# Where VectorE turns blocks of adj, and when norm and x rows are handled, in a four-layer graph network

## The chip, the cores and the metric

One core of a Trainium2 chip runs the whole program. The metric is the device time of one execution in microseconds (us); the number given is the median of several runs.

## The reference

Inputs are x (4096 x 256) and a sparse matrix adj (4096 x 4096), all float32. Four layers each compute x = layernorm(x + layer(x, adj)):

- Layer 0 is attention with 4 heads of 64 columns. `scores = q k^T / 8 + graph_bias * adj`, set to -1e9 where adj is 0, softmax over the row, times v, then an output projection.
- Layer 1 is graph attention with leaky ReLU and a softmax over the edges.
- Layers 2 and 3 multiply by adj scaled by its row sums on both sides, and by a weight matrix.

Layers 2 and 3 need adj transposed, as operand of TensorE. The kernel makes that copy, adjT, in HBM while layer 0 runs.

## The kernel before, in words

The change touches layer 0 (`layer0_attention`, L149 to L974) alone. The rows of the output are cut into 16 chunks of 256 rows (`CT` = 2 tiles of 128). A chunk has 4 heads; a head has 8 beats (`BEATS`), one for each piece of 128 rows by 1024 columns of scores. Four beats are a side (`SIDE`), so a chunk has 8 sides of 4 beats, 32 beats. A pair (side, r) names a beat: side 0 to 7, r 0 to 3. The order of all engines is written out by hand in terms of these pairs, and each engine has its own program:

- **TensorE** (`tensor_program`, L640): in a side it makes the scores of four pieces, 12 beats ahead of their use (L579), turns four pieces of finished probabilities by a multiplication with the identity (L592), and at the end of the side multiplies the turned pieces by the values (`aggregate`, L605, 32 matmuls). In sides with half = 0 it projects the output of the head before (L614). In side 3 it turns the x rows of the next chunk (`turn_x`, L550) and sides 1, 3, 5 and 7 include, for every second head, the making of q (L559). Scores and turned pieces share three PSUM places of two banks in turn; the scores of step r = 0 have to be read before the second turned piece of the side can be written, those of r = 1 before the third scores.
- **VectorE** (`vector_program`, L931): at each beat it reads one piece of scores (`read_scores`, L865: scale, add bias, row maximum, written to SBUF). After it, by (side, r), come the other jobs: at r = 1 the sum of a finished head is inverted, at r = 3 the projected rows are added to `acc` (`add_step`, L903), in sides 4 to 6 the bias of the next chunk is made (`MAKE_BIAS`, L816 and L827/L829), and blocks of adj are turned (`turn_block`, L885).
- **ScalarE** takes the exponential (L716), copies turned pieces out of PSUM (L725) and issues the loads of the values, two of 256 KB a side (L766).
- **GpSimd** (POOL) makes the masks for the bias of the next chunk (L502), takes the power in the layer norm (L129) and stores the finished rows x1 (L494).
- **SyncE** (SP) issues, in the order of its program, the loads of blocks (L393), four stores for each turned block (L403), the loads of x rows (L470, L473) and, at beats 12 to 19 of a chunk, the eight loads of the next chunk's bias of 512 KB each (L382).

**Blocks.** adj is cut into 256 blocks of 128 rows by 512 columns (256 KB). A block is loaded to one of four places (`squares`), turned in place by VectorE in squares of 32 x 32, and written to adjT by four DMAs of 64 KB in pieces of 128 bytes. `BLOCKS_AT` says how many blocks are turned after the read of the beat (side, r); its counts sum to 17 a chunk, so chunk 15 has one block left. SP handles a block one beat behind VectorE (`store_turned`): it waits until block b is turned, issues the four stores, waits until the stores of block b-1 have landed and issues the load of block b+3:

```
for b in blocks_in(c, side, r):
    store_block(b)
    if b + 3 < BLOCKS:
        wait(sync, block_stored[(b + 3) % BLOCK_PLACES], ...)
        load_block(b + 3)
```

**Norm and acc.** When the last head of chunk c-1 has been added at (0, 3) of chunk c, VectorE takes the statistics of `acc` (`ln.statistics`), POOL the power, VectorE normalises in place (`ln.normalise`), and POOL stores the rows. Then `start_acc(c)` (L887) waits for that store and for the x rows of chunk c, and sets acc to x + bo. Behind it SP loads the x rows of chunk c+1 into the same tile `xs`; TensorE turns them in side 3. After that `xs` serves as mask of two wide pieces of bias and is loaded once more in side 7.

Of the kernel before, what the change touches and what calls it, by code (L numbers as in the profile page):

```python
# [39 lines left out]
def wait(eng, sem, value):  # L40

    if isinstance(value, int) and value <= 0:
        return
    eng.wait_ge(sem, value)
# [104 lines left out]
def layer0_attention(nc, shared, x, adj, Wqkv, bqkv, Wout, bout, graph_bias, v_heads, value_stored, x1, x1_stored, adjT):  # L149
# [48 lines left out]
    SCORE_STEP = (0, 2, 5, 7)  # L198
    TURN_STEP = (1, 3, 4, 6)
    SIDE_STEPS = 2 * SIDE  # L200
    BLOCKS_AT = {(0, 1): 1, (0, 3): 2, (1, 3): 3, (2, 1): 1, (2, 3): 2, (3, 1): 1, (3, 3): 1, (6, 3): 2, (7, 1): 1, (7, 3): 3}
    CHUNK_BLOCKS = sum(BLOCKS_AT.values())
    WIDE = (3, 6)
    NARROW = tuple(i for i in range(BEATS) if i not in WIDE)
    x_tiles, adj_tiles, x1_tiles, w_rows = tiles_of(x), tiles_of(adj), tiles_of(x1), tiles_of(Wqkv)
    with ExitStack() as ctx:
# [13 lines left out]
        acc = sp.sb("acc", [P, CT, D])  # L220
# [10 lines left out]
        ln = LayerNorm(sp, CT)  # L231
# [59 lines left out]
        acc_ready = sp.sem("acc_ready")  # L291
# [28 lines left out]
        def x_loads(c, first):  # L320

            return 16 * (2 * c + 1) if c == 0 or not first else 16 * 2 * c

        def is_first(c, h):
            return isinstance(c, int) and c == 0 and h == 0
# [5 lines left out]
        def blocks_in(c, side, r):  # L331

            before = sum(n for slot, n in BLOCKS_AT.items() if slot < (side, r))
            first = CHUNK_BLOCKS * c + before
            return [b for b in range(first, first + BLOCKS_AT.get((side, r), 0)) if b < BLOCKS]

        pool_of_places = (turn_bank[1], turn_bank[0], score_bank)

        def score_place(side, r):

            return pool_of_places[(SIDE_STEPS * side + SCORE_STEP[r]) % 3]
# [5 lines left out]
        def sides():  # L347

            return ((h, half, 2 * h + half, SIDE * half) for h in range(H) for half in range(2))
# [17 lines left out]
        def unit_after(c, h, ahead):  # L367

            return c + (h + ahead) // H, (h + ahead) % H
# [5 lines left out]
        def sync_program(sync, early):  # L375
# [4 lines left out]
            def load_bias(c, i):  # L380
                t, pp = piece_at(i)
                sync.dma_start(bias[:, t:t + 1, pp * PIECE:(pp + 1) * PIECE],  # L382
                               adj_tiles[:, bass.ds(c * CT + t, 1), pp * PIECE:(pp + 1) * PIECE])\
                    .then_inc(adj_loaded[i], 16)
# [62 lines left out]
            def store_turned(c, side, r):  # L447
# [4 lines that stand above are left out]
                        wait(sync, block_stored[(b + 3) % BLOCK_PLACES], 16 * SQUARES * ((b + 3) // BLOCK_PLACES))  # L452
                        load_block(b + 3)

            def body(c, last):
                for h, half, side, j0 in sides():
                    for r in range(SIDE):
                        at = BEATS * h + j0 + r
                        if r:
                            store_turned(c, side, r - 1)  # L460
                        elif side:
                            store_turned(c, side - 1, SIDE - 1)
                        elif c:
                            store_turned(c - 1, SIDES - 1, SIDE - 1)
                        if last:
                            early(sync, at)
                            continue
                        if h == 1 and half == 0 and r == 2:
                            sync.wait_ge(acc_start, CT * (c + 1))
                            sync.dma_start(xs[:], x_tiles[:, bass.ds((c + 1) * CT, CT), :]).then_inc(x_loaded, 16)  # L470
                        if h == H - 1 and half == 1 and r == 1:
                            wait(sync, wide_used, len(WIDE) * (c + 1))
                            sync.dma_start(xs[:], x_tiles[:, bass.ds((c + 1) * CT, CT), :]).then_inc(x_loaded, 16)  # L473
                        if BIAS_LOAD <= at < BIAS_LOAD + BEATS:
                            i = at - BIAS_LOAD
                            sync.wait_ge(score_read, CHUNK_BEATS * c + (H - 1) * BEATS + i + 1)
                            load_bias(c + 1, i)
            chunks(sync, body)

        def gpsimd_program(pool):  # L480
# [301 lines left out]
        def vector_program(dve, early):  # L782
# [104 lines left out]
            def start_acc(c):  # L887

                wait(dve, x1_stored, 16 * c)
                dve.wait_ge(x_loaded, x_loads(c, False))  # L890
                for t in range(CT):
                    dve.tensor_tensor(acc[:, t, :], xs[:, t, :], bo[:], ALU.add).then_inc(acc_start, 1)
# [38 lines left out]
            def body(c, last):  # L931
                for h, half, side, j0 in sides():
                    s = H * c + h
                    before = unit_after(c, h, -1)
                    has_before = not is_first(c, h)
                    G = SIDES * c + side
                    for r in range(SIDE):
                        j = j0 + r + AHEAD
                        if not (last and h + j // BEATS >= H):
                            read_scores(*unit_after(c, h, j // BEATS), j % BEATS, score_place(G, r))  # L940
                        if r == 1:
                            if half == 1:
                                invert_sums(s, h % 2)
                            if side == 1 and has_before and c:
                                dve.wait_ge(acc_ready, s)
                                ln.statistics(dve, acc, c - 1)
                            if side == 2:
                                start_acc(c)
                        if r == 3:
                            if half == 0 and has_before:  # L950
                                add_step(s - 1, before[1], before[1] % 2, before[0])
                            if side == 1 and c:
                                ln.normalise(dve, acc, c - 1)
                            if half == 1 and h % 2 and not (last and h + 3 >= H):
                                for e in range(2):
                                    finish_q(*unit_after(c, h, 3), e)
                        if (side, r) in MAKE_BIAS and not last:
                            i = MAKE_BIAS[side, r]
                            if i in WIDE:
                                make_wide_bias(c + 1, i)  # L960
                            else:
                                make_bias(c + 1, i)
                        for b in blocks_in(c, side, r):
                            turn_block(b)
                        if last:
                            early(dve, SIDE * side + r)
            chunks(dve, body)
            final = UNITS - 1
            add_step(final, H - 1, (H - 1) % 2, CHUNKS - 1)
# [1054 lines left out]
```

## Time and profile before

| | us |
|---|---|
| median of 3 runs | 3180.06 (3180.02 to 3185.33) |
| the profiled execution | 3181.8 |
| its span | 3180.1 |
| TensorE matmul busy | 2997.9 (94%) |
| TensorE weight loads busy | 2212.2 (70%) |
| VectorE busy | 2115.4 (67%) |
| ScalarE busy | 1893.3 (60%) |
| GpSimd busy | 764.6 (24%) |

The profile records one execution. A busy time counts instructions at work; matmuls are pipelined, so a busy TensorE need not be at its peak. Idle time in front of an instruction is put down to what released it. The granted clock is the share of TensorE's full clock that the chip gave. DMA share is the mean busy share of the 16 DMA engines. Layer 0 takes about the first 1760 us of the span, the other layers the rest.

### The profile page before, as it was taken

How to read it: one execution, taken by the hardware profiler on the slowest of the kernel's cores; microseconds unless marked ns; L12 is line 12 of the kernel's file. 1: busy time of each engine (PE TensorE's matmuls, PEld its weight loads, DVE VectorE, ACT ScalarE, POOL GpSimd, SP SyncE). 2: the span in 40 equal slices, each digit the busy share in tenths (PEclk: the TensorE clock that was granted, in tenths of full speed). 3: DMA queues.
4: the chain of work that ended last, by engine and by line, in shares of the span. 5: the costliest groups of instructions: out<-in, count | busy, mean ns of one | idle time of the engine just before them, and what ended most of it. 6: DMA issues, size and time to landing. Idle time of an engine off the chain costs nothing.

```text
span 3180.1 us, 45294 instructions
## 1 busy us (share of the span) xinstructions
PE 2997.9 (94%) x16612; PEld 2212.2 (70%) x16612; DVE 2115.4 (67%) x3607; ACT 1893.3 (60%) x2705; POOL 764.6 (24%) x454
## 2 busy tenths in 40 slices
PE   8898999999999999998999899999999999999998
PEld 6676777776777677776777555555547888788887
DVE  6677767776777677766775797777734554664554
ACT  3666667666666667666767477777754333443332
POOL 2123312331133113321330145555530110000000
PEclk9999999999999999999999999999999999999999
DMA  6788797789787978797775533334248999899882
GB/s 185 145 159 173 174 178 163 173 176 186 157 178 175 189 161 175 168 204 146 170 167 128 206 144 120 146 119 146 84 106 194 217 201 204 212 214 215 204 197 65
DMA packets 725868, 534.42 MB, mean 168 GB/s; under 512 B 565776, under 2 KB 605968, under 8 KB 709264
## 3 DMA queue, kind: packets, MB, share of 16 engines
q1 hardware_dynamic: 682464, 445.00, 61.3%
q10 hardware_dynamic: 36288, 66.08, 8.6%
q0 software_dynamic: 6896, 20.45, 2.2%
q8 instruction: 133, 2.18, 0.3%
q14 instruction: 87, 0.71, 0.1%
HBM read 443.29 MB, written 88.08 MB: 167 GB/s over the span
## 4 chain that ended last, share of the span: by engine, by line
PE 60%; DMA 13%; DVE 12%; SPq 7%; issue 5%; ACT 2%; POOL 1%; DVEq 0%; POOLq 0%; ACTq 0%
PE gl_four L1474 11%; PE gl_quad L1527 7%; PE gl_quad L1528 7%; PE gl_quad L1529 7%; PE at_o L605 5%; DMA adjT<-at_probs 5%; PE at_turn L579 5%; SPq L403 5%; PE at_turn L592 5%; DVE at_probs L865 4%; DMA at_probs<-in_adj 4%; PE gl_quad L1457 3%; PE at_score L579 3%; DVE at_bias L816 2%; PE at_score L592 2%
## 5 line engine op out<-in xcount | busy, mean ns | idle before, releaser
L716 ACT ACTIVATE at_probs<-at_probs,at_minus_max 128x1024 f32<-128x1024 f32 x512 | 581.7, 1139 | 10.7 <-DVE at_minus_max L870 9.8
L725 ACT ACTIVATE at_pT<-at_turn 128x1024 f32<-128x1024 f32 x342 | 346.1, 1024 | 308.8 <-PE at_turn L592 308.6
L865 DVE CUSTOM_DVE_ANT_0 at_probs<-at_turn,at_bias 128x1024 f32<-128x1024 f32 x336 | 409.0, 1220 | 164.2 <-PE at_turn L579 158.3
L502 POOL TENSOR_SCALAR at_masked<-at_bias 128x512 bf16<-128x512 f32 x180 | 374.2, 2093 | 582.2 <-DMA at_bias<-in_adj 535.1
L605 PE MATMUL at_o<-at_pT,at_values 128*64 128x256 f32 x4096 | 470.3, 382 | 0.0
L1474 PE MATMUL gl_four<-gl_early,gl_first_wh 128*128 128x512 f32 x1024 | 462.5, 595 | 6.4 <-ACT gl_early L1595 6.4
L1620 ACT ACTIVATE gl_split<-gl_units 128x1024 fp32r<-128x1024 f32 x256 | 263.8, 1055 | 278.6 <-PE gl_quad L1529 278.6
L592 PE MATMUL at_turn<-all_ident,at_probs 128*128 128x128 f32 x2736 | 366.8, 281 | 56.0 <-DVE at_maxima L865 53.6
L579 PE MATMUL at_turn<-at_kT,at_q 128*128 128x512 f32 x1344 | 403.8, 423 | 10.0 <-DVE at_maxima L865 10.0
L1527 PE MATMUL gl_quad<-gl_split,gl_rows_hi 128*128 128x512 f32 x1024 | 402.4, 393 | 4.7 <-DVE gl_split L1808 4.6
L605 PEld LDWEIGHTS at_o<-at_pT,at_values 128*64 128x64 f32 x4096 | 282.5, 137 | 172.8 <-issue 43.2
L1528 PE MATMUL gl_quad<-gl_split,gl_rows_hi 128*128 128x512 f32 x1024 | 398.5, 389 | 0.0
L1529 PE MATMUL gl_quad<-gl_split,gl_rows_lo 128*128 128x512 f32 x1024 | 398.5, 389 | 0.0
L592 PEld LDWEIGHTS at_turn<-all_ident,at_probs 128*128 128x128 f32 x2736 | 327.0, 145 | 101.9 <-DVE at_maxima L865 68.5
L1808 DVE TENSOR_TENSOR gl_split<-gl_units,gl_split 128x1024 fp32r<-128x1024 f32 x256 | 306.3, 1222 | 116.4 <-ACT gl_split L1620 116.0
L1474 PEld LDWEIGHTS gl_four<-gl_early,gl_first_wh 128*128 128x128 f32 x1024 | 185.2, 191 | 192.4 <-issue 185.2
L885 DVE STREAM_TRANSPOSE at_probs<-at_probs 128x512 f32<-128x512 f32 x256 | 175.5, 700 | 207.7 <-DMA at_probs<-in_adj 206.6
L1170 POOL TENSOR_SCALAR gl_first_weights<-gl_first_weights 128x1024 f32<-128x1024 f32 x57 | 237.2, 4162 | 267.6 <-ACT gl_first_weights L1577 267.6
L579 PEld LDWEIGHTS at_turn<-at_kT,at_q 128*128 128x128 f32 x1344 | 233.0, 193 | 74.7 <-issue 30.7
L865 DVE CUSTOM_DVE_ANT_0 at_probs<-at_score,at_bias 128x1024 f32<-128x1024 f32 x176 | 214.7, 1220 | 90.1 <-PE at_score L579 87.0
L725 ACT ACTIVATE at_pT<-at_score 128x1024 f32<-128x1024 f32 x170 | 174.0, 1024 | 154.9 <-PE at_score L592 154.9
L1527 PEld LDWEIGHTS gl_quad<-gl_split,gl_rows_hi 128*128 128x128 f32 x1024 | 192.3, 188 | 46.6 <-DVE gl_split L1808 6.8
(135 smaller groups left out, 3838.0 us busy)
## 6 DMA issues: line engine op xcount, KB each, us to landing
gl_units<-adjT SPq DMA_DIRECT2D x512, 256.0 KB, 7.8
at_bias<-in_adj SPq DMA_DIRECT2D x128, 512.0 KB, 7.1
at_probs<-in_adj SPq DMA_DIRECT2D x256, 256.0 KB, 4.9
adjT<-at_probs SPq DMA_DIRECT2D x1024, 64.0 KB, 4.4
gl_first_weights<-in_adj SPq DMA_DIRECT2D x32, 2048.0 KB, 8.2
at_values<-v_heads ACTq DMA_DIRECT2D x252, 256.0 KB, 5.1
gl_early<-x SPq DMA_DIRECT2D x160, 128.0 KB, 2.6
x<-gl_early POOLq DMA_DIRECT2D x64, 128.0 KB, 2.7
```

The lines of the kernel that those rows point to most:

```text
L502: pool.tensor_scalar(masked[:, g % MASKS, :], part, 0.0, MASKED / SCALE, ALU.is_equal, ALU.mult)\
L579: last = pe.matmul(place[:, at], q[:, q_place(h), part, t * P:(t + 1) * P], kT[:, h, col:col + BANK], start=part == 0, stop=part == 1)
L592: last = pe.transpose(place[:, a * CN + t * P:a * CN + (t + 1) * P], ring[:, place_in_ring(s, m // BEATS), t, m % BEATS * P:(m % BEATS + 1 ...
L605: last = pe.matmul(o_bank[side * HD:(side + 1) * HD, 0:CN], values[:, q, a, :], pT[:, slot, a % GROUP * CN:(a % GROUP + 1) * CN], start=q ...
L716: act.activation(part, part, ACT.Exp, bias=minus_max[:, k, t:t + 1], scale=1.0, accum_out=sums[:, k, t, pp:pp + 1]).then_inc(prob_ready, 1)
L725: act.activation(pT[:, j % PT_SLOTS, :], place[:], ACT.Copy).then_inc(pT_ready, 1)
L865: dve.tensor_tensor_reduce(out=ring[:, place_in_ring(u, pp), t, :], in0=place[:], in1=bias[:, t, at], scale=SCALE, scalar=LOWEST, op0=ALU. ...
L1474: last = pe.matmul(out_bank1[c % 2][half], wh[:, m * D + half * P:m * D + (half + 1) * P], pT[:, g % PT_RING, part * CN:(part + 1) * CN], ...
L1527: pe.matmul(out_bank3[r % 2][half], rows_hi[:, at], block_hi, start=first, stop=False)
L1528: pe.matmul(out_bank3[r % 2][half], rows_hi[:, at], block_lo, start=False, stop=False)
L1529: last = pe.matmul(out_bank3[r % 2][half], rows_lo[:, at], block_hi, start=False, stop=final)
L1808: dve.tensor_tensor(split3[:, slot, 1, :], tiles[:, n, part:part + 2 * CN], split3[:, slot, 0, :].bitcast(F32), ALU.subtract).then_inc(lo3 ...
```

## The change

It gives `BLOCKS_AT` one block a beat on 17 beats, where it had one to three blocks on ten; the sum stays 17. VectorE's statistics of the finished chunk go from (1, 1) to (0, 3), the normalising from (1, 3) to (1, 1), the start of acc from (2, 1) to (2, 0). SP's load of the next chunk's x rows goes from (2, 2) to (2, 1). The condition `has_before and c` becomes `c`, which is the same for the chunks in question. The loads of the values are as they were, two of 256 KB a side.

```diff
-    BLOCKS_AT = {(0, 1): 1, (0, 3): 2, (1, 3): 3, (2, 1): 1, (2, 3): 2, (3, 1): 1, (3, 3): 1, (6, 3): 2, (7, 1): 1, (7, 3): 3}
+    BLOCKS_AT = {(0, 0): 1, (0, 2): 1, (1, 0): 1, (1, 2): 1, (2, 1): 1, (2, 2): 1, (2, 3): 1, (3, 0): 1, (3, 1): 1, (3, 2): 1, (4, 0): 1, (4, 2): 1, (5, 0): 1, (6, 3): 1, (7, 0): 1, (7, 1): 1, (7, 2): 1}
...
-                        if h == 1 and half == 0 and r == 2:
+                        if h == 1 and half == 0 and r == 1:
                             sync.wait_ge(acc_start, CT * (c + 1))
                             sync.dma_start(xs[:], x_tiles[:, bass.ds((c + 1) * CT, CT), :]).then_inc(x_loaded, 16)
...
                         if r == 1:
                             if half == 1:
                                 invert_sums(s, h % 2)
-                            if side == 1 and has_before and c:
-                                dve.wait_ge(acc_ready, s)
-                                ln.statistics(dve, acc, c - 1)
-                            if side == 2:
-                                start_acc(c)
+                            if side == 1 and c:
+                                ln.normalise(dve, acc, c - 1)
+                        if r == 0 and side == 2:
+                            start_acc(c)
                         if r == 3:
                             if half == 0 and has_before:
                                 add_step(s - 1, before[1], before[1] % 2, before[0])
-                            if side == 1 and c:
-                                ln.normalise(dve, acc, c - 1)
+                            if side == 0 and c:
+                                dve.wait_ge(acc_ready, s)
+                                ln.statistics(dve, acc, c - 1)
```

## Rows read from the trace of the kernel before

**Rows 1.** By stretch: start:end, length; busy PE, PEld, DVE, ACT, POOL; clock; DMA share; GB/s.
```profile
201.80:1678.50 1476.70, 1362.08 (x9352) 1048.39 (x9352) 1041.35 (x1932) 1006.21 (x1472) 370.92 (x196) 0.97 0.83 173
730.90:835.20 104.30, 94.71 (x668) 72.58 (x668) 74.59 (x138) 71.74 (x105) 24.78 (x14) 1.00 0.86 176
```
**Rows 2.** Waits from 100 to 1690 us: us in total, times, longest us.
```profile
PE at_turn L592 <- DVE at_maxima L865: 53.6, 24, 4.6
PE at_mixed L550 <- DMA at_xs<-in_x: 28.6, 14, 4.1
PE at_score L592 <- DVE at_maxima L865: 26.2, 12, 4.1
PE at_turn L579 <- DVE at_maxima L865: 9.4, 10, 1.0
PE at_score L579 <- DVE at_maxima L865: 5.5, 5, 1.7
...
DVE at_probs L885 <- DMA at_probs<-in_adj: 206.6, 99, 5.4
```
**Rows 3.** Timeline, TensorE: start us, us, instruction, [idle before, releaser].
```profile
510.70 1.18 PE L579 MATMUL at_turn<-at_kT,at_q 128*128 128x512 f32 x4
...
523.22 1.09 PE L592 MATMUL at_turn<-all_ident,at_probs 128*128 128x128 f32 x8 [2.16 <-DVE at_maxima L865]
...
548.08 1.09 PE L592 MATMUL at_score<-all_ident,at_probs 128*128 128x128 f32 x8 [1.74 <-DVE at_maxima L865]
...
563.31 1.09 PE L550 MATMUL at_mixed<-all_ident,at_xs 128*128 128x128 f32 x4 [2.27 <-DMA at_xs<-in_x]
564.19 1.91 PE L592 MATMUL at_score<-all_ident,at_probs 128*128 128x128 f32 x8
...
602.19 1.19 PE L579 MATMUL at_turn<-at_kT,at_q 128*128 128x512 f32 x4 [0.98 <-DVE at_maxima L865]
...
1679.79 3.38 PE L592 MATMUL at_turn<-all_ident,at_probs 128*128 128x128 f32 x16 [4.64 <-DVE at_maxima L865]
```
**Rows 4.** Timeline, VectorE, chunk 5 and the end of chunk 4.
```profile
507.57 1.22 DVE L865 CUSTOM_DVE_ANT_0 at_probs<-at_score,at_bias 128x1024 f32<-128x1024 f32 x1 [0.50 <-PE at_score L579]
...
509.34 1.23 DVE L865 CUSTOM_DVE_ANT_0 at_probs<-at_turn,at_bias 128x1024 f32<-128x1024 f32 x1 [0.54 <-PE at_turn L579]
...
521.19 0.71 DVE L885 STREAM_TRANSPOSE at_probs<-at_probs 128x512 f32<-128x512 f32 x1 [2.29 <-DMA at_probs<-in_adj]
...
546.19 0.71 DVE L885 STREAM_TRANSPOSE at_probs<-at_probs 128x512 f32<-128x512 f32 x1 [3.25 <-DMA at_probs<-in_adj]
...
549.09 0.75 DVE L892 TENSOR_TENSOR at_acc<-at_xs,at_bo 128x256 f32<-128x256 f32 x2
...
600.90 1.23 DVE L865 CUSTOM_DVE_ANT_0 at_probs<-at_turn,at_bias 128x1024 f32<-128x1024 f32 x1
```
**Rows 5.** Timeline, SP's queue: first, middle and last issues of the 17 blocks.
```profile
506.51 2.00 SPq L403 DMA_DIRECT2D adjT<-at_probs  x4
...
557.80 0.43 SPq L470 DMA_DIRECT2D at_xs<-in_x  x1
...
579.78 2.52 SPq L393 DMA_DIRECT2D at_probs<-in_adj  x1
```
**Rows 6.** DMA issues: count, KB each, median us to landing; then the range for L393.
```profile
at_probs<-in_adj SPq DMA_DIRECT2D x256, 256.0 KB, 4.9
adjT<-at_probs SPq DMA_DIRECT2D x1024, 64.0 KB, 4.4
...
DMA to landing us min/median/max: 3.3/4.9/9.8
```
**Rows 7.** Instructions on at_acc: landing of POOL's store of x1.
```profile
DMA to landing us min/median/max: 3.4/5.0/6.9
```
**Rows 8.** Busy time by stretch, inside chunk 5, columns as in the first group.
```profile
505.00:585.00 80.00, 73.84 (x514) 57.02 (x512) 54.17 (x107) 54.92 (x82) 12.04 (x8) 0.98 0.98 188
591.00:609.00 18.00, 17.02 (x125) 12.58 (x125) 17.37 (x27) 13.65 (x21) 10.74 (x5) 1.00 0.19 66
```

## The prediction

> **What bounds the kernel now.** I read the stages first. The attention layer runs 16 chunks over the first 1760 us; 14 of them, from the first score read of chunk 1 to that of chunk 15, take 1476.70 us [rows 1], so 105.5 us each. In them TensorE is busy for 1362.08 us, VectorE for 1041.35 and ScalarE for 1006.21: TensorE sets the pace and the reader is to see how little of its time is left, 114.6 us or 8.2 us a chunk. The stages behind, from about 1760 us on, have nothing that the diff touches.
>
> The second view is who waited for whom around the attention layer [rows 2]. TensorE waits 53.6 + 26.2 + 9.4 + 5.5 = 94.7 us for VectorE's read of scores (L865), which frees a PSUM place, and 28.6 us for the DMA of the x rows. VectorE itself waits 206.6 us, in 99 pieces, for a block of adj that it is to turn. So the chain is: block load late, read of scores late, TensorE stalls.
>
> The third is where in a chunk that happens [rows 3, 4]. For VectorE, chunk 5 begins at 521.9, behind the block of 521.19 + 0.71. Four stalls stand there. 523.22, 2.16 us: behind the three blocks of step (7,3), the last of which waited 2.29 us for its load. 548.08, 1.74 us: behind the three blocks of (1,3), the last with a wait of 3.25 us. 563.31, 2.27 us: the x rows, before they are turned. 602.19, 0.98 us: in side 6, where VectorE makes the bias without a pause. The first two places together cost (94.7 - 15 x 1.0) / 15 = 5.3 us a chunk.
>
> The clock is the last part. One chunk ran at a granted clock of 1.00, and there TensorE was busy for 94.71 us [rows 1]; the mean is 1362.08 / 14 = 97.3 us at 0.97. So 2.6 us a chunk is work at the half level of 1.2 GHz, which lies after the stalls: behind the 2.27 us stall eight of the small matmuls take 1.91 us [rows 3], where 1.09 is usual. The Trainium skill (TensorE: Matmul & The Clock Gate, section HAM oscillation) takes half the throttled time as its price; with a mean clock of 0.97 that would be an estimate of 0.03 x 1476.7 = 44 us, 8 more than the 36 us by rows, since a part of the half-clock time is stall and holds no matmul. I go by the rows.
>
> **The blocks.** Before, a chunk's 17 blocks stand on 10 of the 32 beats, up to three at once; after, on 17 beats, one each. Count, work on VectorE (0.71 us each) and bytes stay. What sets when a block is there is the ring of four: the load of block n+3 is issued behind the store of block n, on SP, and behind the landing of store n-1. A block costs SP 2.00 us for its four stores alone; from the first store at 506.51 to the end of the last load (579.78 + 2.52) there are 17 blocks, two loads of x and four of bias, so 4.5 us a block, or an estimate of 4.0 with some 1 us taken off for each of the other loads [rows 5]. Landing takes 4.4 us for a store, 4.9 for a load [rows 6]. Three blocks at one beat therefore ask for 12 us of SP where the next beats give 3 each: these are the waits of 2 to 3 us. With one block to a beat and mostly every second beat (sides 7, 0, 1), a beat being about 3.0 us without stalls, the block n+3 has at least 9 us, minus 2.0 to issue the store and 4.9 to land: 2.1 us of slack, and 5 or more from (0,2) on. The stalls at (7,3) and (1,3) go: that is nearly all of the 94.7 us except 0.98 a chunk in side 6.
>
> The tight place is (2,1) to (3,2), six blocks on six beats, with four of the eight bias loads behind them. At 4.0 to 4.5 us on SP against 3.0 a beat each block is 1.0 to 1.5 us later than the one before: slack 2.1, 1.1, 0.1, or 2.1, 0.6, -0.9 us for (3,0), (3,1), (3,2). The late one is at r = 2, and there VectorE has room: after the last read of a side TensorE multiplies by the values and asks for nothing. At (1,3) 3.25 us of waiting and three blocks of 0.71 made a stall of just 1.74, so 3.25 + 2.13 - 1.74 = 3.6 us were hidden [rows 3, 4]; the read at 507.57, behind an acc step and the two blocks of (6,3), still waits 0.50 us for its scores [rows 4]. A wait at r = 1 to 3 up to some 3 us costs nothing. (4,0) has a beat more and 2 to 3 us of slack.
>
> **Blocks at r = 0.** This is the part that costs. Six of the 17 blocks now stand at r = 0, and the start of acc comes to (2,0). Between the read of the first and of the second scores of a side VectorE has just 0.54 us (507.57 and 509.34) [rows 4]. A block of 0.71 (or acc's two adds, 0.75 together) makes the second read 0.17 to 0.3 us late; it ended at 510.57 and TensorE's third scores began at 510.70 [rows 3]; in side 6, where they wait, they begin 0.06 us after the read's end (602.13 to 602.19), so 0.07 us are to spare. So each costs 0.1 to 0.25 us, or 0 if later matmuls take it up; I take 0.15, seven times: 1.05 us a chunk. (5,0) stands ahead of the bias and may make that stall longer by 0.15 us.
>
> **Norm and start of acc.** The statistics (two passes over acc and three small instructions) go from (1,1) to (0,3), behind the acc step that they need and in place of two blocks. My rows don't price them; I bound them by the two adds over the same tile, 0.75 us, and the two blocks that they replace, 1.42: no more work than was there. The wait for acc_ready is now for VectorE's own last instruction, between 0 and some 0.1 us (0.06 was seen between engines). Queued behind both is the first read of side 1, and the 3.6 us above cover them. POOL's power between statistics and norm has two beats, as before. The normalising goes from (1,3) to (1,1), so POOL's store of x1 starts two beats earlier, and the start of acc, which waits for it, only one: from the norm's end to (2,0) there are some 8 us (three beats less the norm) for POOL's issue and a landing of 5.0 (3.4 to 6.9) [rows 7]. I cost it at 0, and at 1 us a chunk if the issue takes 2 us and the landing the longest.
>
> **The x rows.** SP's load at (2,2) waits for the start of acc (done 549.84) but is issued at 557.80, since the stores of (2,1)'s block and of those before stand ahead of it [rows 4, 5]; it lands at 563.2, TensorE wanted it at 561.05. After, its slot (2,1) has only older stores ahead, all issued by then (no block at (2,0), one each at (1,0) and (1,2)), so it goes out when acc starts: 8 us sooner for the queue and 3 for the beat. It frees 28.6 us in all, and I cost at nothing what it does to the queue: the same 256 KB come ahead of the run of six and not in it. Values stay as they are.
>
> **Sum.** A chunk after: 94.7 busy + 1.0 (side 6) + 0.15 + 1.05 (r = 0) + 1.0 left of block waits + 0.5 of half clock = 98.4 us, 7.1 less than 105.5; times 14 is 99. The last two lie between 0 and the 5.3 and 2.6 that stand there now; I choose near the lower end, since the slacks above are positive. Chunk 15 has one block before and after, at no cost. Chunk 0 gives 3 (one x stall, the longest being 4.1 [rows 2]) and the stall of 4.64 us at 1679.79 [rows 3] with its half clock 5. In all 107 us. The rows are of an execution of 3181.8 us with a span of 3180.1, 1.7 less. The median of the three runs is 3180.06, so the execution was 1.7 above it, and I take 3180.1 - 107 = **3073 us**. With no new cost at all a chunk would be 95.7, the saving 145, the time 3035.
>
> **Rivals.**
> 1. The run of six is later than I make it and the waits reach r = 0 of (3,0) and (4,0), or (0,0): a stall of 2 us at one or two of them each chunk, 3.5 us with its half clock. For it: the DMA engines are at 0.98 from 505 to 585 [rows 8] and a load has taken up to 9.8 us [rows 6]. 107 - 49 = 58: 3122 us. 18%.
> 2. Only the x rows gain; the block waits move to other steps and are as long. 28.6 and some half clock, 40: 3140 us. 7%.
> 3. The transfers are the bound. From 505 to 585 their share is 0.98, then 18 us at 0.19 [rows 8]: if the 83% of a chunk that they take (0.83 x 105.5 = 88 us) can't lie in the idle part, the chunk stays as it is, 3175 to 3180 us. Against it: the last blocks now stand at (4,2) and (5,0), nearer to the idle part; 88 us fit into 98. 4%. The Trainium skill (DMA: Bandwidth & Descriptors, Specifications) wants 512 B or more for full rate; the stores here have 128 B pieces. By that rule the work of the transfers is fixed and the order of the blocks gains nothing, this rival's time.
> 4. Slower: r = 0 decides. Each of the six blocks there has nothing to hide a wait. If each waits as long as the mean of now, 206.6 / 99 = 2.1 us, that is 12.6 us a chunk against 7.1 gained: 14 x 5.5 = 77 us more, 3257 us. It turns at 1.2 us for each. 5%.
>
> **How the numbers follow.** Forecast 66%, the rivals 18, 7, 4 and 5. The range reaches from 3050 (most of the new costs absent) to 3128, which takes in rival 1; the other three, 16%, and a little of either end are outside. 0.2%, some 6 us, is about what a measurement here can tell from none. Faster: 66 + 18 + 7 = 0.91; the same 0.04; slower 0.05.
>
> **What would show it.** Chunks of 98 to 99 us; VectorE's wait for block loads down from 206.6 to under 80 us and mostly at (7,2), (3,1) and (3,2); no wait of TensorE on the x rows; 1 us in side 6 as before; pauses of 0.1 to 0.2 us in front of TensorE's third scores in sides with a block at r = 0; mean clock of the stage 0.99 or 1.00; the stages behind unchanged. Wrong would be: TensorE waits of 2 us and more behind (0,0), (3,0) or (4,0), a wait of VectorE for POOL's store at (2,0), or bias masks that come late, since the bias loads stand behind more stores.

## The result, and the profile after

| | before | after |
|---|---|---|
| median, us | 3180.06 (3180.02 to 3185.33, 3 runs) | 3073.85 (3067.49 to 3087.08, 4 runs) |
| ratio to the kernel before | 1 | 0.9666, interval 0.9625 to 0.9707 |
| profiled execution / span, us | 3181.8 / 3180.1 | 3087.08 / 3085.4 |

One execution of the kernel before (6838.51 us) and one of a kernel below (5161.68 us, the x load one beat later) were in a slow state and are in none of the numbers here. The changed kernel is 3.3% faster, within 1 us of the 3073 forecast; its own executions differ by 20 us. The execution that was profiled is the longest of its four; the same kernel was run again later (below) and profiled at a span of 3070.5. Busy time by stretch, from the first read of chunk 1 to that of chunk 15, as in [rows 1] (columns: start:end, length; busy PE, PEld, DVE, ACT, POOL; clock; DMA share; GB/s):

```profile
196.70:1584.80 1388.10, 1338.55 (x9354) 1035.48 (x9353) 1031.46 (x1932) 999.13 (x1471) 359.25 (x196) 0.98 0.91 184
```

A chunk takes 1388.10 / 14 = 99.15 us where it took 105.5. TensorE's busy time went from 97.3 to 95.6 us a chunk, its idle time from 8.2 to 3.5. The layers behind are as long as before: 94.7 us are missing from the span, and 14 x 6.33 = 88.6 of them lie in these chunks, the rest in the first and the last.

Where in a chunk it went is seen from the starts of VectorE's first reads of each side (mean of the chunks 1 to 14, us, from VectorE's timeline; "second" is the second profile of the changed kernel):

| side | 0 | 1 | 2 | 3 | 4 | 5 | 6 | 7 | chunk |
|---|---|---|---|---|---|---|---|---|---|
| before | 12.5 | 11.6 | 14.5 | 16.0 | 11.9 | 11.2 | 13.0 | 14.7 | 105.5 |
| after | 11.9 | 11.0 | 11.9 | 12.4 | 12.2 | 11.5 | 16.5 | 11.8 | 99.15 |
| after, second | 11.9 | 11.0 | 11.9 | 12.3 | 12.1 | 11.7 | 15.2 | 11.8 | 97.9 |

Sides 0 to 3 and 7 gain 10.4 us together, and side 6 loses 3.5 of that, 2.2 in the second profile. The waits from 100 to 1690 us of the changed kernel, as in [rows 2] (us in total, times, longest):

```profile
DVE at_probs L885 <- DMA at_probs<-in_adj: 74.0, 54, 3.3
DVE at_bias L816 <- POOL at_masked L502: 42.9, 51, 2.5
...
PE at_turn L579 <- DVE at_maxima L865: 30.2, 13, 4.4
PE at_score L579 <- DVE at_maxima L865: 15.5, 8, 3.6
PE at_turn L592 <- DVE at_maxima L865: 6.9, 6, 1.6
PE at_score L592 <- DVE at_maxima L865: 0.8, 1, 0.8
```

TensorE's waits for the read of scores fell from 94.7 to 53.4 us, that for the x rows from 28.6 to nothing, VectorE's wait for blocks from 206.6 to 74.0. One line is new: VectorE waits 42.9 us for POOL's masks. In the kernel before, the whole list has 0.7 us of it. And the waits on L592, in sides 0 and 3 for the most part, have been replaced by waits on L579, in side 6. The timelines of SP's queue, POOL, VectorE and TensorE at such a place (start us, us, instruction, [idle before, releaser]):

```profile
554.95 5.32 SPq L403 DMA_DIRECT2D adjT<-at_probs  x4
560.32 2.65 SPq L393 DMA_DIRECT2D at_probs<-in_adj  x1
563.02 1.78 SPq L382 DMA_DIRECT2D at_bias<-in_adj  x2
...
569.67 3.81 POOL L502 TENSOR_SCALAR at_masked<-at_bias 128x512 bf16<-128x512 f32 x2 [2.58 <-DMA at_bias<-in_adj]
...
571.62 1.08 DVE L816 SCALAR_TENSOR_TENSOR at_bias<-at_bias,at_gain,at_masked 128x512 f32<-128x512 f32 x1 [2.39 <-POOL at_masked L502]
573.51 0.75 DVE L816 SCALAR_TENSOR_TENSOR at_bias<-at_bias,at_gain,at_masked 128x512 f32<-128x512 f32 x1 [0.80 <-POOL at_masked L502]
...
575.59 2.08 PE L579 MATMUL at_turn<-at_kT,at_q 128*128 128x512 f32 x4 [4.33 <-DVE at_maxima L865]
```

SP spends 8 us on the stores and the load of one block (554.95 to 562.97) and only then issues the bias loads of pieces 5 and 6. POOL starts on piece 5 at 569.67, when it lands; VectorE, at (6,0), has been waiting for its masks; TensorE stalls for 4.33 us where [rows 3] had 0.98, and its next matmuls run at the half clock (2.08 us for four where 1.19 is usual).

The blocks at r = 0 can be seen in two pairs of rows, VectorE and TensorE of one side:

```profile
599.76 0.71 DVE L885 STREAM_TRANSPOSE at_probs<-at_probs 128x512 f32<-128x512 f32 x1
600.39 1.18 DVE L865 CUSTOM_DVE_ANT_0 at_probs<-at_turn,at_bias 128x1024 f32<-128x1024 f32 x1
...
599.09 1.17 PE L579 MATMUL at_turn<-at_kT,at_q 128*128 128x512 f32 x4
...
601.77 1.18 PE L579 MATMUL at_turn<-at_kT,at_q 128*128 128x512 f32 x4
```

The read behind the block starts 0.63 us after it and takes 1.18 us instead of 1.23. TensorE's second and third scores are 2.68 us apart. In sides of the kernel before without a block there, the third scores follow at the same distance (508.02 to 510.70; the latter in [rows 3]). Over the chunks 1 to 14 of the changed kernel TensorE never waits for a read of scores in sides 0 to 3. A block at r = 0 that is there in time costs nothing in these rows.

### The profile page after: what moved, and what is told of

It reads as the page before. It is cut to its first block, busy times and chain, and to the rows that moved or that the text cites. A ratio compares the mean times of both kernels' runs of the same rounds, so it can differ in the third digit from the quotient of the medians.

```text
span 3085.4 us, 45294 instructions
## 1 busy us (share of the span) xinstructions
PE 2972.5 (96%) x16612; PEld 2197.6 (71%) x16612; DVE 2104.4 (68%) x3607; ACT 1886.0 (61%) x2705; POOL 752.4 (24%) x454
## 4 chain that ended last, share of the span: by engine, by line
PE 65%; DMA 11%; DVE 6%; issue 6%; SPq 6%; POOL 4%; ACT 2%; POOLq 0%; DVEq 0%; ACTq 0%
PE gl_four L1474 12%; PE at_o L605 8%; PE gl_quad L1527 7%; PE gl_quad L1528 7%; PE gl_quad L1529 7%; PE at_turn L579 6%; PE at_turn L592 5%; DMA at_probs<-in_adj 4%; SPq L403 3%; PE at_score L579 3%; PE gl_quad L1457 3%; POOL at_masked L502 3%; DMA adjT<-at_probs 3%; PE at_score L592 2%; DMA at_bias<-in_adj 2%
## 5 line engine op out<-in xcount | busy, mean ns | idle before, releaser
L502 POOL TENSOR_SCALAR at_masked<-at_bias 128x512 bf16<-128x512 f32 x180 | 362.0, 2024 | 647.4 <-DMA at_bias<-in_adj 642.3
L579 PE MATMUL at_turn<-at_kT,at_q 128*128 128x512 f32 x1344 | 404.4, 423 | 30.6 <-DVE at_maxima L865 30.4
L592 PE MATMUL at_turn<-all_ident,at_probs 128*128 128x128 f32 x2736 | 354.8, 276 | 9.4 <-DVE at_maxima L865 6.9
L592 PEld LDWEIGHTS at_turn<-all_ident,at_probs 128*128 128x128 f32 x2736 | 319.1, 142 | 49.1 <-DVE at_maxima L865 12.2
L579 PEld LDWEIGHTS at_turn<-at_kT,at_q 128*128 128x128 f32 x1344 | 232.6, 193 | 96.7 <-DVE at_maxima L865 37.7
L579 PE MATMUL at_score<-at_kT,at_q 128*128 128x512 f32 x704 | 212.6, 424 | 18.8 <-DVE at_maxima L865 18.7
```

The source lines that it names most:

```text
L502: pool.tensor_scalar(masked[:, g % MASKS, :], part, 0.0, MASKED / SCALE, ALU.is_equal, ALU.mult)\
L579: last = pe.matmul(place[:, at], q[:, q_place(h), part, t * P:(t + 1) * P], kT[:, h, col:col + BANK], start=part == 0, stop=part == 1)
L592: last = pe.transpose(place[:, a * CN + t * P:a * CN + (t + 1) * P], ring[:, place_in_ring(s, m // BEATS), t, m % BEATS * P:(m % BEATS + 1 ...
```

## The experiments

All were compared with the kernel before on the chip that they ran on; its median there was 3185.46 us for the change once more, the two halves and the bias loads first, 3185.29 for the late x load, the two blocks at r = 0 and the blocks out of sides 4 and 5, 3182.6 for the first three of the blocks moved behind the bias loads, and 3189.53 for the last kernel. What is said of one kernel against another goes by the ratios to these.

**The changed kernel once more.**

> The changed kernel itself, once more, so that the others of this batch can be held against it. All theories: about 3074 us (3067 to 3087), TensorE's waits for the read of scores at 3 us a chunk, nearly all in side 6, and VectorE waiting some 40 us in all for POOL's masks.

Measured: 3073.17 us, ratio 0.9653 (0.9627 to 0.9679). A chunk takes 97.9 us here, TensorE busy 94.9 of them, 3.0 idle. The stretch:

```profile
196.80:1567.30 1370.50, 1328.79 (x9355) 1026.33 (x9353) 1034.15 (x1932) 999.17 (x1471) 364.01 (x196) 0.99 0.92 186
```

and its waits:

```profile
DVE at_probs L885 <- DMA at_probs<-in_adj: 62.7, 55, 2.9
DVE at_bias L816 <- POOL at_masked L502: 39.0, 57, 1.8
```

**The two halves alone.** Only the blocks spread:

```diff
-    BLOCKS_AT = {(0, 1): 1, (0, 3): 2, (1, 3): 3, (2, 1): 1, (2, 3): 2, (3, 1): 1, (3, 3): 1, (6, 3): 2, (7, 1): 1, (7, 3): 3}
+    BLOCKS_AT = {(0, 0): 1, (0, 2): 1, (1, 0): 1, (1, 2): 1, (2, 1): 1, (2, 2): 1, (2, 3): 1, (3, 0): 1, (3, 1): 1, (3, 2): 1, (4, 0): 1, (4, 2): 1, (5, 0): 1, (6, 3): 1, (7, 0): 1, (7, 1): 1, (7, 2): 1}
```

> Only the blocks are spread; statistics, norm, start of acc and x rows stay where they were. Theory (the parts add up, the x rows are a wait of their own): the block stalls go and the x stall of about 2 us a chunk stays or shrinks to 1, since fewer stores stand ahead of the load on SP: 3085 to 3105 us. Rival (spreading the blocks alone frees SP so early that the x rows come in time and the moves are worth nothing): 3070 to 3080 us, no wait of TensorE on the x rows.

Only statistics, norm, start of acc and x rows moved (the change without this line):

> Only statistics, norm, start of acc and x rows are moved; the blocks stay in their clusters. Theory: TensorE's 28.6 us on the x rows go, the 5 us a chunk behind (7,3) and (1,3) stay: 3145 to 3160 us. Rival (the moves help only together with the spread blocks, since a stall removed in side 3 comes back behind the clusters, which SP and the DMA engines serve no faster): 3165 to 3182 us.

Measured: blocks alone 3094.44 us, ratio 0.9723 (0.9697 to 0.9749), moves alone 3130.46 us, 0.9832 (0.9794 to 0.987). Against 3185.46 that is 91 and 55 us, 146 together, where both at once give 112. Waits with the blocks alone:

```profile
DVE at_probs L885 <- DMA at_probs<-in_adj: 121.5, 78, 3.5
...
PE at_mixed L550 <- DMA at_xs<-in_x: 0.6, 1, 0.6
```

With the moves alone:

```profile
DVE at_probs L885 <- DMA at_probs<-in_adj: 196.8, 94, 6.0
...
PE at_turn L592 <- DVE at_maxima L865: 52.6, 26, 5.7
```

The time of the first lies in the theory's range, but its mechanism was the rival's: with the blocks spread, the x rows come in time without being moved (0.6 us of waiting in all). What the moves add shows on the blocks: without them VectorE waits 121.5 us for block loads, with them 62.7. The moves alone gave more than the 25 to 40 us expected, though the block waits stayed (196.8; L592 as in [rows 2]): TensorE's waits for VectorE and x rows fell from 123.3 to 52.6 + 19.9 + 16.6 + 7.7 = 96.8, and the mean clock of the chunks rose from 0.97 to 0.98. By side, side 3 is 3.8 us shorter than before and side 2 is 0.8, while sides 0, 6 and 7 are 1.4 longer together: the gain lies around the place of the x rows, where the stall behind the blocks of (2,3) shrank with it. The parts of that gain weren't run one by one.

**The place of the x load.** The changed kernel with only this undone:

```diff
-                        if h == 1 and half == 0 and r == 1:
+                        if h == 1 and half == 0 and r == 2:
```

> The changed kernel with SP's load of x rows back at (2,2); statistics, norm and start of acc as in the change. Theory (what the early slot is worth beside spread blocks is that the load does not stand in the run of six): block waits grow by 20 to 60 us in all, TensorE does not wait for x rows, 3080 to 3095 us. Rival (the 20 us between spread blocks alone and the whole change come from the norm and acc steps on VectorE): 3070 to 3077 us.

Measured: 3086.34 us, 0.9694 (0.9678 to 0.971), in the range of the theory. Block waits are 90.9 us, 28 more than with the load at (2,1), and TensorE waits once for x rows, 1.5 us. So of the 21 us between the blocks alone and the whole change, some 13 are the slot of the x load (the two intervals just touch): one beat later it stands behind the store of (2,1), at the head of the run of six blocks. This kernel and the one with the blocks alone differ in just the statistics, norm and start of acc; the 8 us between them are within the intervals.

**Bias loads first.** SP issues the bias load of a beat ahead of the stores and the load of the block turned one beat earlier:

```diff
                     for r in range(SIDE):
                         at = BEATS * h + j0 + r
+                        if not last and BIAS_LOAD <= at < BIAS_LOAD + BEATS:
+                            i = at - BIAS_LOAD
+                            sync.wait_ge(score_read, CHUNK_BEATS * c + (H - 1) * BEATS + i + 1)
+                            load_bias(c + 1, i)
                         if r:
                             store_turned(c, side, r - 1)
...
-                        if BIAS_LOAD <= at < BIAS_LOAD + BEATS:
-                            i = at - BIAS_LOAD
-                            sync.wait_ge(score_read, CHUNK_BEATS * c + (H - 1) * BEATS + i + 1)
-                            load_bias(c + 1, i)
```

> The changed kernel with SP issuing the bias load of a beat ahead of the stores and the load of the turned block, where it issues it behind them. Theory (side 6 stalls for 2.7 us a chunk because the bias loads stand behind block stores on SP and the masks come late): the wait of VectorE for masks falls from 43 to under 10 us, side 6 to 1.0 us a chunk, and some block waits grow but are hidden: 3045 to 3060 us. Rival 1 (the DMA engines are full there, so the order on SP only says which transfer is late; block waits at (3,1) to (4,0) grow as much): 3070 to 3080 us. Rival 2 (side 6 is bound by VectorE's work, the block at (5,0) included): no change of the stall.

Measured: 3093.92 us, 0.9723 (0.9693 to 0.9753), 20 us worse than the change. Half of the theory holds: the waits for masks are gone from the list, and side 6 is down to 12.9 us. But block waits grew from 62.7 to 116.7 us, as rival 1 had it, and cost more than the masks had: those at (4,0) and (5,0) are at r = 0, with nothing to hide them, and sides 3 to 5 are 3.5 us a chunk longer. VectorE at (3,2), (4,0) and TensorE behind it:

```profile
545.60 0.71 DVE L885 STREAM_TRANSPOSE at_probs<-at_probs 128x512 f32<-128x512 f32 x1 [4.26 <-DMA at_probs<-in_adj]
...
550.66 1.97 PE L592 MATMUL at_turn<-all_ident,at_probs 128*128 128x128 f32 x16 [1.97 <-DVE at_maxima L865]
...
553.15 0.71 DVE L885 STREAM_TRANSPOSE at_probs<-at_probs 128x512 f32<-128x512 f32 x1 [2.54 <-DMA at_probs<-in_adj]
...
555.04 1.19 PE L579 MATMUL at_score<-at_kT,at_q 128*128 128x512 f32 x4 [2.41 <-DVE at_maxima L865]
```

**Two blocks at r = 0.**

```diff
-    (0, 0): 1, (0, 2): 1, (1, 0): 1, (1, 2): 1,
+    (0, 0): 2, (1, 0): 2,
```

> The changed kernel with the blocks of (0,2) and (1,2) moved to (0,0) and (1,0), so two blocks stand at r = 0 of sides 0 and 1. Theory (one block at r = 0 is free, because it fits the 0.54 us pause and the next read needs no wait; the room ends there): sides 0 and 1 grow by 0.4 to 0.7 us each where they had not grown at all, 1 us a chunk or 16 us in all: 3085 to 3095 us. Rival (the PSUM places give more room than that): no change, 3070 to 3078 us.

Measured: 3123.66 us, 0.9803 (0.9775 to 0.983), 50 us worse than the change. Of VectorE and TensorE in side 0 of one chunk:

```profile
499.69 1.35 DVE L885 STREAM_TRANSPOSE at_probs<-at_probs 128x512 f32<-128x512 f32 x2
500.97 1.19 DVE L865 CUSTOM_DVE_ANT_0 at_probs<-at_turn,at_bias 128x1024 f32<-128x1024 f32 x1
...
499.02 1.17 PE L579 MATMUL at_turn<-at_kT,at_q 128*128 128x512 f32 x4
...
502.22 1.19 PE L579 MATMUL at_turn<-at_kT,at_q 128*128 128x512 f32 x4 [0.28 <-DVE at_maxima L865]
```

The second and third scores are 3.20 us apart instead of 2.68: the second block costs 0.52 us, as the theory had it; that is 1 us a chunk. Most of the rest is another effect, which the expectation lacked: the second block's load wasn't always there. In eight of the chunks 1 to 14 VectorE waited at (0,0), 0.4 to 5.4 us, 18.8 in all, where nothing hides it. The chunks 1 to 14 are 42 us longer than in the change's second profile: side 0 takes 33 of that (the block and the lateness), side 1 7 (the block), side 6 5. The execution profiled was the shortest of its four (3108.43 us); what the others, up to 3128.77, have on top isn't known.

**Two blocks taken out of sides 4 and 5.**

```diff
-    (0, 0): 1, (0, 2): 1, (1, 0): 1, (1, 2): 1,
+    (0, 0): 1, (0, 2): 1, (0, 3): 1, (1, 0): 1, (1, 2): 1, (1, 3): 1,
...
-    (4, 0): 1, (4, 2): 1, (5, 0): 1,
+    (4, 0): 1,
```

> The changed kernel with the blocks of (4,2) and (5,0) moved to (0,3) and (1,3). Theory (SP and the DMA engines are overfull only in sides 2 to 5, where bias loads come too, and have room in sides 0 and 1): the waits for masks fall from 39 us to under 20, side 6 to 1.0 to 1.5 us a chunk, 3050 to 3065 us. Rival (sides 0 and 1 have no room, the run of six then begins with a backlog and its block waits reach (4,0)): 3073 us or more.

The same blocks with the bias loads first:

> The kernel with two blocks moved to (0,3) and (1,3), and the bias loads ahead of the stores of their beat. Theory (with the bias first the lateness falls on block loads, and with two blocks fewer in sides 4 and 5 there is less to be late, but (4,0) is still at r = 0): masks wait under 5 us in all, stalls at (4,0) 1 to 2 us a chunk, 3065 to 3080 us, not better than the same blocks without it. Rival (two blocks fewer are enough for both): 3045 to 3055 us.

Measured: 3118.68 us, 0.9794 (0.978 to 0.9809), and 3122.62 us, 0.9801 (0.9784 to 0.9817). Both theories fell; the first kernel is 45 us worse than the change. The rival of the first is what its trace shows: the run of six begins with a backlog, the block of (4,0), at r = 0, waits in nine chunks (in two of the change's second profile), 9.5 us in all, and sides 3 and 4 are 1.5 us a chunk longer. Side 6 is 1.0 us longer as well. Mask waits stayed at 34.7 us and TensorE's stall in side 6 grew from 2.2 to 3.6 us a chunk; in the second kernel they fell to 2.0 us, and block waits rose to 141.8. The issue times of the bias loads show what happened to the masks. Mean over the chunks 1 to 14, from the timelines of SP and VectorE: us after VectorE's read at (3,0), and how far ahead of the read of the beat at which the mask is used:

| kernel | piece 5, used at (6,0): issued, ahead | piece 7, used at (6,2): issued, ahead |
|---|---|---|
| before | 24.5, 14.6 | 25.8, 19.6 |
| the change | 30.3, 5.8 | 37.6, 6.6 |
| the change, second profile | 29.7, 6.4 | 36.8, 6.7 |
| blocks at (0,3), (1,3) for (4,2), (5,0) | 32.1, 5.8 | 33.3, 12.8 |
| block of (4,0) at (4,1) | 22.3, 13.8 | 37.5, 4.9 |
| and that of (4,2) at (4,3) | 22.3, 13.7 | 32.2, 10.4 |

A bias load of 512 KB takes 6.3 us to land in the changed kernel (median), and POOL needs some 4 us for the two masks behind it, so 6 us ahead is late and 10 isn't. Piece 5 is issued at beat 17, behind the block of (4,0) (beat 16) and ahead of those of (4,2) and (5,0). Taking the latter two away took nothing out of its way; put earlier, they made the blocks of side 3, and piece 5 behind them, some 2 us later. Piece 7 did get out early: its waits at (6,2) went, and those at (5,3) and (6,0) grew.

**Blocks moved behind the bias loads.** That gave the next ones. All take the change and move the block of (4,0) to (4,1), which in SP's order is behind the load of piece 5:

> The changed kernel with the block of (4,0) moved one beat to (4,1). SP's order by beats then has the bias load for piece 5 ahead of this block's stores and load, where it stood behind them. Theory (side 6 waits for the mask of piece 5, made at (6,0), and only what SP issues ahead of that bias load counts: that is why two blocks taken from behind it and put ahead of it cost 45 us): it is issued 4 to 6 us earlier, the wait for masks falls from 39 to under 12 us, side 6 to about 1.0 to 1.3 us a chunk, 3050 to 3062 us. Rival 1 (the transfers as a whole are full between sides 2 and 5; what the masks gain the blocks lose): 3070 to 3080 us. Rival 2 (a block beside the bias work of (4,1) makes VectorE late): a stall of 0.5 us or more a chunk in side 4, 3075 to 3085 us.

With the block of (3,2) at (3,3) as well:

> As the kernel before in this batch, and the block of (3,2), which waits longest for its load, moved to (3,3) as well. Theory (of the same queue): the block waits at (3,2) of 1.3 us a chunk shrink, but they were hidden; no more than 5 us better than the kernel before it, 3047 to 3060 us. Rival: the two writes of q at (3,3) and a block together end too late for the first scores of side 4, a stall there of 0.5 us or more a chunk, 8 us or more above it.

And with that of (5,0) as a second one at (6,3) instead:

> The block of (4,0) at (4,1), and the block of (5,0) as second one at (6,3), where the DMA engines have been idle and two blocks stood before the change. Theory: (6,3) is behind the bias work and its two blocks fit ahead of side 7, so nothing is lost there, and side 5 has 0.7 us less work on VectorE: 0 to 6 us better than with (4,1) alone, 3046 to 3060 us. Rival (the block at (5,0) gave the queue its rest: with two at (6,3) and three more in side 7 the load for (7,2) is late and then for (0,0), which stands at r = 0): stalls of 1 us or more a chunk behind (7,2) and (0,0), 3065 to 3090 us.

Measured: 3070.81 us (0.9647, 0.9605 to 0.9689), 3077.14 us (0.9665, 0.9627 to 0.9703) and 3104.6 us (0.975, 0.9714 to 0.9786).

The first is no faster than the change. It did what it should to piece 5, 8 us earlier, and the wait at (6,0) is 0.7 us or none. But piece 7 wasn't helped, and the wait went there, two beats on:

```profile
562.90 0.75 DVE L816 SCALAR_TENSOR_TENSOR at_bias<-at_bias,at_gain,at_masked 128x512 f32<-128x512 f32 x1 [0.67 <-POOL at_masked L502]
...
571.15 1.08 DVE L816 SCALAR_TENSOR_TENSOR at_bias<-at_bias,at_gain,at_masked 128x512 f32<-128x512 f32 x1 [2.74 <-POOL at_masked L502]
573.03 0.75 DVE L816 SCALAR_TENSOR_TENSOR at_bias<-at_bias,at_gain,at_masked 128x512 f32<-128x512 f32 x1 [0.80 <-POOL at_masked L502]
```

In the second, mask waits fell to 11.2 us, and the block of (5,0), at r = 0, took over: 0.7 to 5.1 us in 13 of the chunks, one of them here with the stall behind it:

```profile
556.72 0.71 DVE L885 STREAM_TRANSPOSE at_probs<-at_probs 128x512 f32<-128x512 f32 x1 [3.37 <-DMA at_probs<-in_adj]
...
558.61 2.07 PE L579 MATMUL at_turn<-at_kT,at_q 128*128 128x512 f32 x4 [3.24 <-DVE at_maxima L865]
```

In the third the rival held: with two blocks at (6,3) those at (7,1) and (7,2) wait for their loads in every chunk, 2.0 to 3.8 us and 0.8 to 3.9.

Three kernels in which a wait only changes its place suggest that queue and engines are simply full there, and the last kernel has that as its rival. It moves the block of (4,2) to (4,3), so that piece 7 gets out of the queue too:

```diff
-    (4, 0): 1, (4, 2): 1, (5, 0): 1,
+    (4, 1): 1, (4, 3): 1, (5, 0): 1,
```

> The block of (4,0) at (4,1) and that of (4,2) at (4,3), so that SP has all eight bias loads ahead of the last three blocks' stores but one. Theory A (only the order on SP counts; with (4,1) alone the mask of piece 5 came in time and the wait went on to that of piece 7, which this removes too): waits for masks under 20 us, stalls of sides 6 and 7 together at 1.0 to 1.3 us a chunk instead of 2.4, 3050 to 3062 us. Theory B (between sides 2 and 5 queue and DMA engines are full, so what comes earlier makes something else late): the wait goes on to the block of (5,0), which stands at r = 0, 2 us and more in most chunks, 3065 to 3080 us.

Measured over five rounds: **3039.23 us** (3037.17 to 3047.84), 0.9551 (0.9531 to 0.9572). It is the best version of this study, 1.1% below the change, and the intervals are well apart. Its chunks, in the view by stretch:

```profile
191.60:1534.90 1343.30, 1318.16 (x9355) 1021.84 (x9354) 1026.98 (x1933) 998.26 (x1471) 369.55 (x196) 1.00 0.93 190
```

The waits from 100 to 1690 us of this kernel:

```profile
DVE at_probs L885 <- DMA at_probs<-in_adj: 37.4, 29, 3.7
PE at_turn L579 <- DVE at_maxima L865: 16.1, 12, 3.3
PE at_score L579 <- DVE at_maxima L865: 8.8, 6, 2.1
DVE at_bias L816 <- POOL at_masked L502: 8.5, 14, 0.7
```

VectorE waits 8.5 us for masks in all, and 37.4 for blocks. A chunk takes 95.95 us, of which TensorE is busy for 94.2 at a clock of 1.00. Against the kernel with only the first of the two moves, 2.0 us a chunk are gone: 1.6 in side 6, 0.3 in side 7, where the waits for piece 7 stood.

Of theory B one half fell: the wait didn't go on to the block of (5,0), which waited in three of the 14 chunks, where 2 us and more in most of them were expected. Its other half, that the DMA engines are full between sides 2 and 5, stands. One chunk in the view by stretch, first from the read at (2,1) to that at (6,0), then side 6; the first two rows are of the change's second profile, the last two of this kernel:

```profile
906.43:953.32 46.89, 45.50 (x327) 35.12 (x326) 35.96 (x66) 34.84 (x52) 16.45 (x9) 1.00 0.97 208
953.32:968.68 15.36, 13.14 (x94) 10.20 (x92) 12.18 (x19) 8.66 (x13) 7.30 (x4) 1.00 0.72 167
890.94:936.41 45.47, 45.47 (x329) 35.35 (x328) 36.32 (x66) 34.82 (x52) 17.26 (x9) 1.00 0.98 211
936.41:949.80 13.39, 12.02 (x85) 8.95 (x83) 11.32 (x20) 8.39 (x12) 7.30 (x4) 1.00 0.80 183
```

As means of the 14 chunks the DMA share of the first stretch is 0.97 in both kernels, against 0.89 before any change. That of side 6 goes from 0.71 to 0.80, against 0.21 before. So within the full stretch one transfer can only come earlier if another comes later, and the order decides which; by these shares, the time was gained because the ones put back could use side 6, where the engines had room.

## Why the prediction was right

The mechanism was right: spread out, the block loads come in time, and TensorE's stalls behind them go. That the sum came out right to 1 us is luck. Two of its terms were wrong by 1 us a chunk and more, and they cancelled, and the four executions differ by 20 us. By its own steps:

- **Block stalls.** Gone, as forecast. But the second place was read from a single chunk (from 521.9 on, chunk 4 if the one at 201.80 is chunk 1) that isn't typical. Of the kernel before, in chunk 1:

```profile
241.06 0.71 DVE L885 STREAM_TRANSPOSE at_probs<-at_probs 128x512 f32<-128x512 f32 x1 [5.44 <-DMA at_probs<-in_adj]
...
242.95 1.97 PE L592 MATMUL at_turn<-all_ident,at_probs 128*128 128x128 f32 x8 [4.03 <-DVE at_maxima L865]
```

  This is the second block of (2,3), with TensorE's stall in side 3. In the chunks 1 to 14 TensorE waited 32.8 us behind (7,3), 33.5 behind (2,3), in eleven of them, and 5.7 behind (1,3). A wait at r = 3 is thus not free up to 3 us, as the step on hidden waits had it: waits of 3.6 to 5.4 us there gave stalls of 3.7 to 4.6, and even those of 1.7 to 2.5 up to 1.3. The sum is untouched, since it took the places together from the total.
- **The waits left.** VectorE's wait for blocks is 74.0 us, under the 80 named, and stands for the most part at (4,2), (3,2), (3,1) and (7,2), places with room; the first of these, with 23 us, wasn't among those named. Outside side 6 some 0.8 us a chunk reach TensorE in the profiled execution, for a term of 1.0.
- **Blocks at r = 0.** 1.05 us a chunk was written down; it is 0. The step set a block of 0.71 us against a pause of 0.54. In a row without a wait the read starts 0.63 us behind the start of the block, and takes 0.05 less: 0.04 us late in all, within the 0.07 us that were to spare. What the step said of the place was right all the same: a second block costs 0.52, and a load that is late there costs all of its lateness.
- **Side 6.** 1.0 + 0.15 us was written down; it was 2.7 in the profiled execution and 2.2 in the second one, and the half clock behind it comes on top. This is the step that failed. The prediction named late bias masks as a sign of being wrong, but had no term for them: it followed the block loads through SP's queue and not the bias loads behind them. Piece 5 went out 14.6 us ahead of its use before and 5.8 after, as its load is issued 6 us later and VectorE is at (6,0) 3 us sooner. SP's time per block isn't the reason: the four stores take 2.8 us in the mean of these chunks before and 2.7 after.
- **x rows.** Right: no wait. But their 28.6 us weren't a sum of their own. Spreading the blocks alone frees them as well; what the early slot gives is 13 us of shorter block waits.
- **Norm and start of acc.** No wait of VectorE for POOL's store or power in these chunks, and none that the profile shows for acc_ready. Right at nothing within the noise: these three alone make the difference between 0.9723 (blocks alone) and 0.9694 (x load late), with intervals that overlap.
- **Half clock.** 0.5 us a chunk; 0.9 in the profiled execution (95.6 - 94.7) and 0.2 in the second.
- **First and last chunk.** 3 and 5 us were written down. Up to the first read of chunk 1 it is 5 us less, and from that of chunk 15 on 1.0 less in the profiled execution and 1.6 more in the second. The 4.64 us stall at 1679.79 was counted twice: the read that ends it starts at 1678.50, which is where the stretch of 14 chunks ends, so all but the end of the stall lies inside it.
- **Sum.** 98.4 us a chunk, measured 99.15 and 97.9. For the whole, 107 us; measured 94.7 between the profiled executions and 109.6 to the second one.

Rival 1 (waits at r = 0 of (3,0), (4,0) or (0,0)) shows in single chunks only, up to 1.0 us at (4,0), and up to 2.5 at (5,0). Rivals 2 and 4 didn't come true; the fourth is what two blocks at (0,0) and (1,0) bring about, on a smaller scale. Rival 3, that the transfers bound the whole chunk, is out: the share of the DMA engines rose from 0.83 to 0.91, and to 0.93 in the last kernel, at the same bytes in less time. What is true of it is the stretch from (2,1) to (6,0), full at 0.97. With the rival falls the Trainium skill's limit of 512 B (DMA: Bandwidth & Descriptors, Specifications) as a reason for no gain; that the 128 B stores are slow for their bytes no run here refutes.

## What to carry to other kernels

When transfers of several kinds share one issuing queue, follow each kind through it to its deadline, not just the one that waits now: a load is late by all that is issued ahead of it, and moving work that stands behind it does nothing. Read where a stall stands from all repetitions of a loop, not from one. Spread work one piece at a time, but put it where its own lateness is hidden; here two beats decided between free and 50 us. And if a wait only moves from one place to the next, look how full the resource is stretch by stretch: here it was full for half of the chunk and had room right behind, and the next step in the same direction brought some 30 us.

## What was unexpected of the hardware

- The issue of the same four stores on SP takes 2.00 us at 506.51 of the kernel before [rows 5], where the DMA share of the 6.5 us ahead of it was 0.10, and 5.32 us at 554.95 of the changed kernel, at a share of 0.93; the single load behind it 2.65 us, where 0.35 to 0.5 is seen elsewhere. All that stands behind in SP's queue waits for it. In the changed kernel the four take 2.1 us in the median where the share is under 0.6, and 2.7, up to 6.1, where it is above 0.9. Some take 1.9 there too, so a busy set of engines goes with long issues, but what makes one long isn't shown.
- VectorE's turning of a block costs 0.63 us, not the 0.71 that its row shows, if the next instruction needn't wait (599.76 to 600.39), or 0.64 a piece for two in a row (1.35 in all, the read at 1.28).
